# A macaron block on one core: feed-forward phases rewritten from 128 tokens with tokens on partitions to 512 tokens with features on partitions

## The reference, cut to what matters

```
x = x + 0.5 * ffn(layernorm(x))
x = x + attn(layernorm(x))             # 16 heads, causal, not touched by the change
x = x + 0.5 * ffn(layernorm(x))

ffn(x), for each of 2 layers:
  h = shift_token(x)                   # upper 64 features come from the token before
  q, k, v = split(h @ wqkv)            # 8 heads of 64
  q, k = l2norm(q) * q_scale, l2norm(k) * k_scale
  q, k = rotary_xpos(q, k)             # x*cos*s + rotate_half(x)*sin*s (k: divided by s)
  sim = 8 * q @ k.T                    # windows of 64 queries, keys of this and the last window, causal
  x = x + softmax(sim) @ v @ wo
  h = layernorm(shift_token(x)) * ln_g + ln_b
  a, g = split(h @ w1 + b1)            # 341 each
  x = x + (a * gelu(g)) @ w2 + b2
```

## Time and profile before

| | us |
|---|---|
| median of 3 timed runs | 2400.47 (2398.17 to 2400.76) |
| the profiled execution's own time | 2398.42 |
| its span, first to last instruction | 2396.6 |
| first bn_stats to the latent phase | 42 to 975 |
| latent phase | 975 to 1453 |
| second feed-forward phase | 1453 to 2392 |

### The profile page before, as it was taken

How to read it: one execution, slowest core, us unless ns; L and a number is a source line. 1 busy time by engine, 2 the same in 40 slices (tenths; PEclk the granted TensorE clock), 3 DMA queues, 4 the chain that set the end, 5 groups by cost and what they waited for, 6 DMA issues and landing times. The chain is left out here.

```text
span 2396.6 us, 58054 instructions
## 1 busy us (share of the span) xinstructions
PE 2115.1 (88%) x20074; PEld 1660.4 (69%) x20074; DVE 2178.8 (91%) x5128; ACT 1672.6 (70%) x3681; POOL 1235.7 (52%) x1036
## 2 busy tenths in 40 slices
PE   2888899889888888799999996999888898888888
PEld 2677777777777777466666664777777777777776
DVE  4999999999999999688888887999999999999997
ACT  1677666776677667488888894667667676767665
POOL 3665556655656555222232225565655665565553
PEclk9999999999999999899999998999999999999999
DMA  3000000000000000000000000000000000000000
GB/s 109 2 2 1 2 2 2 2 1 2 2 2 2 1 2 2 1 2 2 1 2 1 2 2 1 1 2 1 2 1 2 2 2 6 6 6 6 6 6 11
DMA packets 12756, 12.35 MB, mean 5 GB/s; under 512 B 1413, under 2 KB 11703, under 8 KB 12471
## 3 DMA queue, kind: packets, MB, share of 16 engines
q1 hardware_dynamic: 12471, 8.63, 1.2%
HBM read 6.53 MB, written 2.10 MB: 4 GB/s over the span
## 5 line engine op out<-in xcount | busy, mean ns | idle before, releaser
L849 POOL TENSOR_TENSOR RN<-SS,mhalf 128x16 f32<-128x16 f32 x128 | 373.8, 2921 | 9.5 <-DVE SS L723 9.4
L840 POOL TENSOR_TENSOR U2B<-U,b_s 128x128 f32<-128x128 f32 x128 | 61.7, 482 | 584.3 <-DVE U L729 577.1
L541 ACT ACTIVATE PR<-bank,NMX 128x128 f32<-128x128 f32 x1024 | 290.1, 372 | 49.2 <-DVE NMX L634 45.6
L598 ACT ACTIVATE GL<-bank,b_s 114x128 f32<-114x128 f32 (+1 forms) x384 | 113.2, 366 | 258.0 <-PE bank L388 258.0
L379 PE MATMUL bank<-KT,QZ 128*64 128x128 f32 x4096 | 280.1, 279 | 0.0
L379 PEld LDWEIGHTS bank<-KT,QZ 128*64 128x64 f32 x4096 | 218.3, 136 | 70.2 <-issue 70.2
L1094 ACT ACTIVATE PL<-bank,NM 128x384 f32<-128x384 f32 (+3 forms) x512 | 255.8, 540 | 14.2 <-DVE NM L1172 11.4
L1172 DVE TENSOR_REDUCE NM<-bank 128x1 f32<-128x384 f32 (+3 forms) x352 | 217.6, 634 | 35.6 <-PE bank L1008 31.7
L388 PE MATMUL bank<-HN,w_s 128*114 128x128 f32 (+1 forms) x1536 | 222.0, 281 | 0.0
L1017 PE MATMUL bank<-cst,PL 128*128 128x128 f32 x1280 | 199.7, 275 | 3.2 <-DVE PTL L1181 1.1
L364 PE MATMUL bank<-wqkv_h,HTH 128*128 128x512 f32 x384 | 194.7, 507 | 5.7 <-DVE HTL L709 5.7
(11 more groups left out here) (158 smaller groups left out, 6230.8 us busy)
## 6 DMA issues: line engine op xcount, KB each, us to landing
X<-in_L_attn_x SPq DMA_DIRECT2D x8, 256.0 KB, 4.6
out<-X SPq DMA_DIRECT2D x8, 256.0 KB, 2.3
wqkv_raw<-in_L_ffn_wqkv SPq DMA_DIRECT2D x1, 1536.0 KB
w_s<-in_L_ffn_w SPq DMA_DIRECT2D x1, 682.0 KB
rope<-shape_constants SPq DMA_DIRECT2D x1, 512.0 KB
wo_s<-in_L_ffn_wo SPq DMA_DIRECT2D x2, 256.0 KB
cst<-shape_constants SPq DMA_DIRECT2D x1, 259.0 KB
w_s<-in_L_ffn_w SPq DMA_DIRECT2D x2, 114.0 KB
```

The lines of the kernel that those rows point to most:

```text
L541: last = nc.scalar.activation(PR[:, 4 * g + h, :], BK[B_S[g]][:, h * P:(h + 1) * P], ACT.Exp, bias=NMX[:, 4 * g + h:4 * g + h + 1], scale=8.0)
L849: nc.gpsimd.tensor_tensor(RN[:, u % 2, :], SS[:, :], mhalf[:, 0:2 * NH], ALU.pow).then_inc(S["rn_ok"], 1)
```

## The change

Both feed-forward phases are written anew. A unit is now a whole sequence of 512 tokens in one layer: 16 units a phase, 23 loop steps, in each of which pieces of units n+2 to n-4 are done. Activations lie with features on partitions and tokens along the free axis.

- Q and K come out of `project` already with features on partitions, in eight banks of 128 rows x 512 tokens (four pairs m, each with the first and the second halves of the heads' features), so the rotary turn is a combination of two banks. DVE makes the four products of a pair in two instructions of 1024 elements, POOL subtracts and adds.
- The squares' sums per head are a matmul with a selection matrix. The norm's inverse root is exp(-0.5 ln) on ACT with one Newton step on DVE; 16 rows of it go by DMA to DRAM and come back broadcast over 128 partitions; POOL multiplies.
- `scores` gives keys x queries, in tiles of 32 rows by 64 columns, four heads at a time (g = 0, 1). The maximum over 32-key blocks is one `tensor_reduce` with `apply_transpose` a bank; PE transposes the 64 maxima, DVE reduces and spreads them, and PE adds minus the maximum to the scores' banks (`add_max`). The exponentials then need no transpose.
- The softmax sums are a matmul with ones, their inverse exp(-ln) on ACT; it goes to DRAM and back broadcast. The values of the odd windows are copied into `V1` by DMA.
- The layer norm's variance goes through ln, exp, a Newton step and DRAM in the same way. w1 is applied with three single-pass matmuls instead of one in fp32.
- The setup loads larger tables, no longer builds `ropet`, and splits w1 as well.

In the new loop body a line such as `run(scores, n - 1, 0)` does that piece for unit n-1. The core of the diff (the engine's name behind a # is added here):

```
...
+                        def norms(u):
+                            sp.wait_ge(S["nw_ok"], u + 1)
+                            sp.dma_start(norms_d[u % 2], RN[0:P:8, :]).then_inc(S["r_out"], 16)
+                            sp.wait_ge(S["r_out"], 16 * (u + 1))
...
+                            for i in range(4):
+                                src = norms_d[u % 2].rearrange("(c i) n -> i c n", i=4)[i]
+                                sp.dma_start(SQ[32 * i:32 * i + 32, :, 1, :],
+                                             src.unsqueeze(0).broadcast_to([32, 4, T])).then_inc(S["r_in"], 16)
...
+                        def sums(u, g):
+                            n = 2 * u + g
+                            sp.wait_ge(S["dl_ok"], n + 1)
+                            sp.dma_start(sums_d[n % 2], DR[0:P:32, :]).then_inc(S["d_out"], 16)
+                            sp.wait_ge(S["d_out"], 16 * (n + 1))
...
+                            for e in range(2):
+                                src = sums_d[n % 2].rearrange("(j e) n -> e j n", e=2)[e]
+                                sp.dma_start(OT[W * e:W * e + W, 2 * g:2 * g + 2, :],
+                                             src.unsqueeze(0).broadcast_to([W, 2, T])).then_inc(S[("d0_in", "d1_in")[g]], 16)
...
+                        for n in range(-2, NU + 5):                      # SP
+                            run(result, n - 5)
+                            run(sums, n - 1, 0)
+                            run(sums, n - 1, 1)
+                            run(norms, n)
+                            run(variances, n - 2)
+                            run(values, n)
...
+                        def scores(u, g):                                # PE
+                            pe.wait_ge(S["nr_ok"], 4 * u + 2 * g + 2)
+                            for i in range(4):
+                                claim(i, "ex_ok", 8 * u + 4 * g + i + 1)
+                                nc.tensor.matmul(BK[i][:, :], identb[:, :], bandb[:, :], start=True, stop=False,
+                                                 skip_group_check=True)
+                            for t in range(NT):
+                                for z in range(2):
+                                    for e in range(2):
+                                        k0 = (2 * t + e) * W
+                                        n = min(2 * W, T - k0)
+                                        for i in range(4):
+                                            r = slice(32 * i, 32 * i + 32)
+                                            last = nc.tensor.matmul(
+                                                BK[i][e * W:(e + 1) * W, k0:k0 + n], QK[r, 2 * g + 1, z, k0:k0 + W],
+                                                QK[r, 2 * g, z, k0:k0 + n], start=False, stop=(z == 1),
+                                                skip_group_check=True)
...
+                            run(hidden, n - 4, 0, 1, 7)
+                            run(project, n, 0)
+                            run(hidden, n - 4, 0, 2, 6)
+                            run(scores, n - 1, 0)
+                            run(outward, n - 4, 6)
+                            run(turn_max, n - 1, 0, 7)
+                            run(project, n, 1)
+                            run(add_max, n - 1, 0)
+                            run(join, n - 2, 7)
+                            run(project, n, 2)
+                            run(scores, n - 1, 1)
+                            run(sums, n - 1, 0, 7)
+                            run(project, n, 3)
+                            run(turn_max, n - 1, 1, 6)
+                            run(center, n - 2, 7)
+                            run(add_max, n - 1, 1)
+                            run(norms, n, 6)
+                            run(variance, n - 2, 5)
+                            run(attend, n - 1, 0, 7)
+                            run(sums, n - 1, 1, 4)
+                            run(hidden, n - 3, 1, 0, 6)
+                            run(attend, n - 1, 1, 7)
...
+                            run(values, n, 3, 7)
+                            run(hidden, n - 3, 0, 0, 4)
...
+                        def norms(u):                                    # ACT
...
+                            link(nc.scalar.activation(RN[:, :], VN[:, :], ACT.Ln))
+                            nc.scalar.activation(RN[:, :], RN[:, :], ACT.Exp, scale=-0.5).then_inc(S["rl_ok"], 1)
...
+                            run(softmax_exp, n - 1, 0)
+                            run(square_b, n, 1)
+                            run(square_a, n, 2)
+                            run(square_b, n, 2)
+                            run(sums, n - 1, 0, 7)
+                            run(square_a, n, 3)
+                            run(high_hidden, n - 3)
+                            run(square_b, n, 3)
+                            run(square_c, n - 2, 7)
+                            run(softmax_exp, n - 1, 1)
+                            run(norms, n)
+                            run(sums, n - 1, 1, 4)
+                            run(gate, n - 3, 0, 6)
...
+                            run(variance, n - 2)
+                            run(values, n, 0, 5)
+                            run(values, n, 1, 4)
...
+                        def rotate(u, m, z):                             # DVE
...
+                                    dve.wait_ge(S["ad_ok"], 4 * u + m)
...
+                            nc.vector.scalar_tensor_tensor(
+                                out=TP[:, o:o + 2, :], in0=BK[4 + z][:, :].unsqueeze(1).to_broadcast([P, 2, T]), scalar=q,
+                                in1=tab[:, e, :, :], op0=ALU.mult, op1=ALU.mult).then_inc(S[("na_ok", "nb_ok")[z]], 1)
...
+                        def maxima(u, g):
...
+                            for i in range(4):
+                                last = nc.vector.tensor_reduce(MX[:, i, :], BK[i][:, :].rearrange("p (a b) -> p a b", b=32),
+                                                               AX_X, ALU.max, apply_transpose=True)
...
+                            run(maxima, n - 1, 1)
+                            run(rotate, n, 3, 1)
+                            run(spread_max, n - 1, 1, 6)
+                            run(rotate, n, 3, 0)
+                            run(clamp, n, 6)
+                            run(attended, n - 1, 0, 7)
+                            run(add_eps, n - 2, 5)
+                            run(norms, n)
+                            run(attended, n - 1, 1, 7)
+                            run(attended, n - 1, 2, 7)
...
+                        for n in range(-2, NU + 5):                      # POOL
+                            run(tokens, n + 2)
+                            run(low, n)
+                            run(norms, n - 1, 1)
+                            run(norms, n - 1, 2)
+                            run(norms, n - 1, 3)
+                            run(rotate, n, 0)
+                            run(hidden, n - 3)
+                            run(rotate, n, 1)
+                            run(rotate, n, 2)
+                            run(low_hidden, n - 3)
+                            run(rotate, n, 3)
+                            run(norms, n, 0)
...
```

More of the change, by code:

```diff
@@ L56, in macaron @@
     NS = NB * NT
+    assert T == 512 and C == P
     QL = W_dq.shape[0]
@@ L359, in project @@
-                        def project(u, k):
-                            l, bb, t, s = unit(u)
-                            tok, cols = slice(t * P, (t + 1) * P), slice(k * 512, (k + 1) * 512)
-                            for n, (h, w) in enumerate(((HTH, wqkv_h), (HTH, wqkv_l), (HTL, wqkv_h))):
-                                last = nc.tensor.matmul(BK[B_QKV[k]][:, :], h[:, bb, tok].bitcast(F32R),
-                                                        w[:, l, cols].bitcast(F32R), start=(n == 0), stop=(n == 2))
-                            return last
@@ new lines, in values @@
+                        def values(u, t, k):
+                            l = u // NB
+                            pe.wait_ge(S["htl_ok"], u + 1)
+                            claim(k, "ve_ok", 4 * u + t + 1)
+                            for n, (h, w) in enumerate(((HTH, wqkv_h), (HTH, wqkv_l), (HTL, wqkv_h))):
+                                last = nc.tensor.matmul(BK[k][:, :], h[:, t * P:(t + 1) * P].bitcast(F32R),
+                                                        w[:, l, 2 * NH * DH:3 * NH * DH].bitcast(F32R),
+                                                        start=(n == 0), stop=(n == 2))
+                            last.then_inc(S["v_in"], 1)
@@ new lines, in norms @@
+                        def norms(u, k):
+                            pe.wait_ge(S["sa_ok"], 4 * (u + 1))
+                            pe.wait_ge(S["sb_ok"], 4 * (u + 1))
+                            claim(k, "cl_ok", u + 1)
+                            for z in range(2):
+                                for m in range(4):
```

(19 more changed lines are left out.)

1053 lines of the change are left out of this document (491 added, 562 removed).

## The result

| us | before | after |
|---|---|---|
| median | 2399.32 (2397.47 to 2400.76) | 2490.38 (2485.48 to 2492.76) |
| ratio, 95% interval | | 1.0377 [1.0359, 1.0395] |
| span of the profiled execution | 2396.6 | 2488.5 |
| to the first bn_stats | 42.1 | 46.1 |
| feed-forward, latent, feed-forward | 933.3, 478.0, 943.2 | 980.2, 478.0, 984.2 |

The change makes the kernel 3.8% slower; I had forecast 2321, which is 3.3% faster. All of it is in the two rewritten phases (+46.9, +41.0) and 4.0 in the setup; the latent phase is where it was.

What follows compares the result with a forecast made beforehand. DVE bound the old kernel; in the new one waits between engines decide. A phase was 54 + 15 x 51 + 75 = 894 us, two 1788 against 1872; with setup +5 the span was 2317.6, the time 2321, 8-in-10 range 2120 to 2560.

Steps and rivals of the forecast that it cites:

- the order gelu, ln, exp needs two a unit if one table set holds both: ACT's table loads: two a unit, ln then exp costing one load, against 122 and 124 loads of 1.28 us before.
- those two hide behind waits: ACT: a table load runs ahead of its activation's own wait, so two loads a unit add nothing to the sum.
- rival 1: ln and exp from different table sets: nine loads a unit, period 54.5 us, 2443 us in all; chance 0.30.
- The path: Chain of waits from one unit's first scores to the next one's, through the norms' DMA and POOL: period 51.0 us.
- each group of scores: PE's 128 fp32 records and four masks per g: 4.4 us taken, between 2.7 and 7.9.
- the norms' sums: PE's sums for the norms after add_max: 4 slots of 0.43 us, ending at 26.9.
- the transfers: Norms' DMA round trip through DRAM: out until 36.6 us, back in 4 DMAs of 256 KB, last landing at 41.9.
- the half clock's 2.6 us: PE at half clock after waiting for low(n+1): 2.6 us more, taking the period from 48.4 to 51.0.
- The transposing maximum: DVE's maximum over the scores: taken at 0.68 us like the existing form, twice that as upper end, +5 a unit.
- The edges: Fill and drain of each feed-forward phase: 54 us to the first scores, 75 us from the last unit's first scores.
- rival 2: PE-bound: scores at 2.7 us, DMA landings at 2.3, clock up; period 43, 2064 us in all; chance 0.17.
- Rival 3: Row tiles don't overlap and the transposing maximum costs double: period 63 us, 2698 us in all; chance 0.15.

Runs made afterwards that it cites:

- run 1: Kernel after, with the table set holding ln and exp requested at the start and after each unit's gelus: 2375.73 us, 0.9902 of before.
- run 3: run 1 with the norms sent before the second sums in SP's queue: 2457.51 us, 1.0253 of before.
- run 9: run 1 with the norms' DRAM round trip replaced by four fp32 selector matmuls on PE and DVE copies: 2202.42 us, 0.9187 of before.
- run 8: run 1 with the row-tile loop outermost in scores, so neighbouring matmuls share a row tile: 2879.8 us, 1.2015 of before.
- run 5: run 1 with POOL's low(n+1) moved ahead of norms(n, 0): 2368.4 us, 0.9883 of before.
- run 6: run 5 with the second sums' DMAs issued by ACT instead of SP: 2382.52 us, 0.9928 of before.

## Why the prediction was wrong

**The step that failed** is "the order gelu, ln, exp needs two a unit if one table set holds both", and the sentence that those two hide behind waits. The condition was not met: with no set asked for, each ln and each exp after it had a load of its own. The Trainium skill (ScalarE: Activation LUTs, Table sets) says that ln then exp costs one load. One set does hold both, as run 1 shows, but the kernel after loaded for each of the two every time; the measurement decides. The kernel before has no ln, so no row of it could tell; rival 1 stood at 0.30 and the page alone had kept it below the forecast. Its difference to the forecast was 122 us (2443 - 2321); measured 115.

The time is 169 us above the forecast: these 115, and 55 by which run 1, with the loads as forecast, is above 2321. So the loads made the sign wrong, and the size was wrong without them too: a gain of 1% where I had 3.3%.

**The path.** The forecast's order of waits held at each point: POOL on the norms' DMA, PE on HTL with the clock down, two issues of OT ahead of the norms. Times from the start of scores(n-1, 0), in the unit of after shown above (553.48) and the one of run 1 (574.05), whose loads are as the forecast had them:

| | forecast | run 1 | after |
|---|---|---|---|
| norms' exp ends | 28.9 | 28.3 | 29.7 |
| second sums' exp ends | 30.7 | 30.6 | 33.6 |
| norms out, issue | 34.0 | 33.6 | 36.6 |
| norms out, landed | 36.6 | 37.3 | 40.1 |
| SQ landed | 41.9 | 44.6 | 47.0 |
| next scores | 51.0 | 52.1 | 54.4 |

Up to the DMAs the sum is right within 0.6 us, and that is in part luck: each group of scores took 2.9 us with its masks and not 4.4, but the norms' sums took 2.85 instead of 1.8, and DVE's way from the second maxima to add_max 3.1 instead of 2.3. Behind that the transfers are mis-sized: 3.7 us for the norms to be out instead of 2.6, with OT's broadcasts in flight ahead of them (1.9 in run 3, where the norms go first), and 7.3 to the last landing of SQ instead of 5.3. Then it is 7.5 to the next scores instead of 9.1. POOL's norms and low take 3.4 of it, not 4.0. And my sum has a mistake of its own: it adds the half clock's 2.6 us behind norms(n, 1) at 48.4, but PE's project starts when low is done, at 45.9, and runs beside norms(n, 1); by my own terms scores start at 45.9 + 4.2 = 50.1, not 51.0. The errors nearly cancel, which is luck again. The transposing maximum takes 685 ns, as taken.

**The edges** were mis-sized: fill 58.0 and 60.1 us in run 1 against 54, drain 85.9 and 91.7 against 75. That makes 37 us, and the period's 0.85 x 30 steps makes 25; together 63 of phases, less 4 by which I had taken the old phases too short and 1 for setup and latent phase, is the 58 between the forecast's span (2317.6) and that of run 1 (2375.1). I had added up work there; which waits make up the rest no run tried.

**The rivals.** Rival 1's nine loads are what happened, though one set could have held both functions; its period was 54.5, measured 55.5. Of rival 2's conditions the scores came true (2.9 against 2.7), the landings not (medians of 4.6 for SQ and 3.9 for OT against 2.3); with the norms' round trip gone, run 9 reaches 46 where it had 43. Rival 3 needed row tiles that don't overlap; run 8 shows its price.

## What to carry to other kernels

When a rewrite takes the load off the busiest engine, the time can be set by the longest loop from one unit to the next; write it out, with every DMA round trip and table load on it, before counting engine work. Where activations of two functions alternate, count the loads in the trace, and ask for the common set by name. Sending a few rows out to DRAM and back as four broadcasts of 256 KB put 15 us between two dependent steps, selector matmuls with copies 3.5; an edit that fills PE's idle time is worth something only as long as PE waits there; and a mean over steps hides which layer's path an edit touched.

## What the runs showed of the hardware

- Matmuls of 32 x 64 tiles, each row tile with a bank of its own, overlap over row tiles when these are neighbours in PE's queue: 2.03 us for 128, and 6.34 when they aren't (run 8).
- The granted clock fell to 0.50 behind 6.3 us of small matmuls without a gap, not only behind a wait (run 8).
- An 8 KB transfer issued behind 1 MB in the same queue took 4.2 us instead of 1.7 (run 3). With the second sums on a second queue SQ landed 3.1 us earlier and OT 2.2 later than in run 5 (run 6).
- The transposing maximum of 128 x 512 takes 685 ns in after, the plain one 682 in before.
- Each table load takes 1283 ns, and an activation whose input is ready begins within 20 ns of its end (after, 579.34 to 587.06).
